# A graph network on one core: deeper edge gather and prefetch, one-word table look-ups in the edge counts, and 16-bit sums in the second edge pass

## The reference, cut to what matters

```python
# x: 3125 nodes x 128, src and dst: 100000 edges, sorted by dst
# layer 0, edge network
h = relu(batchnorm(concat(x[src], x[dst]) @ W1.T + b1))     # statistics over the edges
u = relu(batchnorm(h @ W2.T + b2))
x = layernorm(x + segment_sum(u, dst))
# layer 1, two graph convolutions, along the edges and against them
x = layernorm(x + relu(gcn(x, W_fwd, src, dst) + gcn(x, W_bwd, dst, src)))
# layer 2, four rounds over the edges
h = relu(x @ Wi.T + bi)
for _ in range(4):
    h = h + relu(tanh(aggregate(h @ Weff.T) - relu(h @ (A - A.T).T)))
x = layernorm(x + h)
# layer 3, attention over the edges with 8 heads
x = layernorm(x + attention(x, src, dst) @ Wo.T + bo)
```

## Time and profile before

| what | value |
|---|---|
| median of 3 runs | 4950.45 us (4930.15 to 4968.29) |
| the profiled execution, its own time | 4959.78 us |
| its span, first to last instruction | 4958.1 us |
| PE, DVE, ACT, POOL busy | 3568.6, 2845.3, 1415.5, 935.4 us |
| mean granted TensorE clock | 0.823 of full speed |
| moved by DMA | 657.34 MB, 133 GB/s over the span |

### The profile page before, as it was taken

How to read it: one execution, slowest core, us unless ns; L and a number is a source line. 1 busy time by engine, 2 the same in 40 slices (tenths; PEclk the granted TensorE clock), 3 DMA queues, 4 the chain that set the end, 5 groups by cost and what they waited for, 6 DMA issues and landing times. The chain is left out here.

```text
span 4958.1 us, 85336 instructions
## 1 busy us (share of the span) xinstructions
PE 3568.6 (72%) x18891; PEld 1725.9 (35%) x18992; DVE 2845.3 (57%) x5040; ACT 1415.5 (29%) x1948; POOL 935.4 (19%) x1131
## 2 busy tenths in 40 slices
PE   3666665557787359998887777447779947778994
PEld 2222222243444237777544333312222212222222
DVE  6887777464333123344101111459989949998993
ACT  1123333301222012222101111121138842117880
POOL 2555555454344421111000000100000000000000
PEclk8988889768999679999898999655569975558996
DMA  2344455528998433332484888262213372213331
GB/s 71 110 143 163 171 181 187 185 92 282 318 317 294 146 121 102 97 89 85 93 243 98 189 190 185 53 87 53 53 49 118 126 106 64 53 26 110 116 110 29
DMA packets 808846, 657.34 MB, mean 133 GB/s; under 512 B 599017, under 2 KB 686184, under 8 KB 808516
## 3 DMA queue, kind: packets, MB, share of 16 engines
q1 hardware_dynamic: 677642, 361.12, 27.7%
q10 hardware_dynamic: 106050, 243.93, 14.9%
q0 software_dynamic: 25088, 51.43, 4.0%
HBM read 316.58 MB, written 196.24 MB: 103 GB/s over the span
## 5 line engine op out<-in xcount | busy, mean ns | idle before, releaser
L621 POOL DMA_INDIRECT gat<-a_table,gidx x784 | 791.5, 1010 | 350.8 <-issue 192.4
L1333 DVE CUSTOM_DVE_ANT_0 masked<-psum,mask 128x1564 bf16<-128x1564 f32 x400 | 698.9, 1784 | 196.0 <-PE psum L1670 188.0
L1670 PE MATMUL psum<-qp,kp 96*128 96x391 bf16 x1600 | 589.7, 524 | 304.8 <-DVE mx L1333 158.4
L1368 DVE SCALAR_TENSOR_TENSOR pw<-ex,c_full 128x1564 f32<-128x1564 f32 x400 | 680.8, 1782 | 48.4 <-ACT ex L942 29.8
L1427 PE MATMUL psum<-one_src,one_dst 128*128 x1968 | 455.5, 370 | 306.2 <-issue 151.9
L942 ACT ACTIVATE ex<-psum 128x782 f32<-128x782 f32 x800 | 609.8, 826 | 77.5 <-PE psum L1692 60.7
L1101 DVE TENSOR_SCALAR one_src<-iota_sub,src_low 128x800 f16 x984 | 430.1, 437 | 187.0 <-issue 97.9
L1475 PE MATMUL psum<-c_ring,hp 128*128 128x512 bf16 (+1 forms) x2064 | 422.6, 360 | 77.6 <-DMA c_ring<-c_parts 55.2
L1670 PEld LDWEIGHTS psum<-qp,kp 96*128 x1600 | 174.3, 129 | 719.7 <-issue 719.7
L1256 DVE TENSOR_SCALAR ohd<-iota,dst_c x976 | 221.8, 299 | 327.4 <-PE psum L1596 282.6
L1427 PEld LDWEIGHTS psum<-one_src,one_dst 128*128 x1968 | 197.7, 104 | 569.7 <-issue 504.6
(11 more groups left out here) (318 smaller groups left out, 3379.7 us busy)
## 6 DMA issues: line engine op xcount, KB each, us to landing
c_full<-c_whole SPq DMA_DIRECT2D x80, 977.5 KB, 5.0
a_edges<-gat SPq DMA_DIRECT2D x196, 256.0 KB
a_in<-a_edges ACTq DMA_DIRECT2D x98, 512.0 KB
r_edges<-r ACTq DMA_DIRECT2D x98, 512.0 KB
r_in<-r_edges SPq DMA_DIRECT2D x98, 512.0 KB, 3.5
c_whole<-c_sum ACTq DMA_DIRECT2D x100, 400.0 KB
dst_bc<-dst_half ACTq DMA_DIRECT2D x98, 256.0 KB
c_parts<-c_hi ACTq DMA_DIRECT2D x100, 200.0 KB
```

The source lines that it names most:

```text
L621: g.indirect_dma_start(gat[:, s, 2 * k * P:2 * (k + 1) * P], None, a_table, bass.IndirectOffsetOnAxis(ap=gidx[:, s, k:k + 1], axis=0)).the ...
L1333: v.tensor_tensor_reduce(out=masked[:, n % 2, :].rearrange("p (c t) -> p c t", c=4), in0=psum[:, o:o + 4 * BANK].rearrange("p (c t) -> p c ...
L1368: v.scalar_tensor_tensor(pw[:, step_slot(k), :].rearrange("p (h t) -> p h t", h=HQ), ex[:, step_slot(k), :].rearrange("p (h t) -> p h t", ...
L1670: last = t.matmul(bank((n % 2) * 4 + c, CW), kp[0:KQK, n // 2, ds(b * P, P)], qp[0:KQK, n // 2, ((n % 2) * 4 + c) * CW:((n % 2) * 4 + c + ...
```

## The change

1. **Gather.** In rounds 24 to 48 POOL waits for the group two before instead of the one before, so eight transfers may be under way. The first 24 rounds are as before.
2. **Counts, table.** Preparation packs end and first of a window in one word (`block_tab` row 3). DVE and PE load this word alone and work out the count of pairs done from the window before, for three windows in four; the first of each four loads a second word. ACT loads none: PE sends `window_done` with a one-column matmul of zeros behind each window.
3. **Counts, one-hot.** The two `one_dst` operations of a pair become one `scalar_tensor_tensor` of 256 elements, with two inputs in SBUF.
4. **Pass 1.** `a_in` and `dst_bc` get four buffers, and each load is issued for unit u+4. The loop's body covers four units instead of two.
5. **Pass 2.** `ohd` becomes f16, four buffers, made by one `tensor_tensor` of 1024 elements with two inputs in SBUF. `u` becomes two f16 parts: ACT writes the high part, and a new DVE operation (`low_part`) writes the rest from PSUM; PE waits for that one (`low_ready`). A visit is 16 f16 matmuls with `ohd` as weights, and its sum comes out turned; at the end 25 matmuls turn `y` back. A bound on the values, found in preparation, scales them into the range of f16.
6. Names of semaphores are merged.

```diff
+        a_in = sb("a_in", [P, 4, UE // P, 2, P], f16)
+        u = sb("u", [P, 2, UE // P, 2, P], f16)
+        ohd = sb("ohd", [P, OHD, UE // P, P], f16)          # OHD = 4
...
+        def window(eng, w, done_pairs):
+            word = eng.value_load(block_tab[0:1, 3, ds(w, 1)], min_val=0, max_val=NPAIR * 512 + NPAIR)
+            first = nc.s_assert_within(eng.snap(word & 511), 0, NPAIR - 2)
+            end = nc.s_assert_within(eng.snap(word >> 9), 2, NPAIR)
+            if done_pairs is None:
+                before = eng.value_load(block_tab[0:1, 2, ds(w, 1)], ...)
+            else:
+                before = nc.s_assert_within(eng.snap((done_pairs - first) & 65535), ...)
+            return first, end, before
...
-            def gather(i):
+            def gather(i, most):
                 for s in range(4):
                     after(pool, gat_free[s], i)
-                    after(pool, gathered[(s + 3) % 4], 64 * i + (64 if s >= 1 else 0))
+                    after(pool, gathered[(s - most) % 4], 64 * i + (64 if s >= most else 0))
...
-            gather(0)
-            with pool.Fori(1, NG // 4) as i:
-                gather(i)
+            gather(0, 1)
+            with pool.Fori(1, SLOW_GATHER) as i:              # SLOW_GATHER = 24
+                gather(i, 1)
+            with pool.Fori(SLOW_GATHER, NG // 4) as i:
+                gather(i, 2)
...
             def evict(i, q):
                 w = 4 * i + q
-                before = act.value_load(block_tab[0:1, 2, ds(w, 1)], ...)
-                end = act.value_load(block_tab[0:1, 1, ds(w, 1)], ...)
-                act.wait_ge(S["slot_free"], before + end + PAIRS)
+                act.wait_ge(S["window_done"], w + 1)
...
-                    last = v.tensor_scalar(one_dst[:, ds(slot, 1), t, :], iota_row[:, :],
-                                           row_c[:, ds(p * 2 + t, 1)], window_at[:, ds(w, 1)],
-                                           ALU.subtract, ALU.is_equal)
+                v.scalar_tensor_tensor(one_dst[:, ds(slot, 1), :, :],
+                                       row_c[:, ds(p * 2, 2)].broadcast_to([P, 2, P]),
+                                       window_at[:, ds(w, 1)],
+                                       iota_row[:, :].broadcast_to([P, 2, P]),
+                                       ALU.add, ALU.is_equal).then_inc(S["one_ready"], 1)
...
+                    t.matmul(bank(2 * (q % 2), 1), zerosb[:, 0:P], zerosb[:, 0:1], start=False, stop=True,
+                             skip_group_check=True).then_inc(S["window_done"], 1)
...
+            def low_part(i, s):
+                dve.wait_ge(h2_taken[4], 2 * i + s + 1)
+                v.scalar_tensor_tensor(u[:, s, :, 1, :], psum[:, s * UE:(s + 1) * UE], 0.0, u[:, s, :, 0, :],
+                                       ALU.max, ALU.subtract).then_inc(S["low_ready"], 1)
...
-                        for k in range(UE // P):
-                            last = v.tensor_scalar(ohd[...], iota[:, ds(b * P, P)],
-                                                   dst_c[:, ds(g * (UE // P) + k, 1)], None, ALU.is_equal)
+                    v.tensor_tensor(ohd[:, ds((before + b) & (OHD - 1), 1), :, :],
+                                    iota[:, ds(b * P, P)].broadcast_to([P, UE // P, P]),
+                                    dst_h[:, ds(g * (UE // P), UE // P)].broadcast_to([P, UE // P, P]),
+                                    ALU.is_equal).then_inc(S["agg_ready"], 1)
...
                     for k in range(UE // P):
-                        last = t.matmul(bank(4, P), u[:, s, k * P:(k + 1) * P], ohd[...], ...)
+                        for m in range(2):
+                            last = t.matmul(bank(4, P), ohd[:, ds((before + b) & (OHD - 1), 1), k, :],
+                                            u[:, s, k, m, :], ...)
...
+            pe.wait_ge(S["sums_ready"], 1)
+            for b in range(NB):
+                last = t.matmul(psum[:, b * P:(b + 1) * P], y[:, b * P:(b + 1) * P], identf[:, :], start=True, stop=True)
+            last.then_inc(S["sums_turned"], 1)
```

More of the change, by code:

```diff
@@ L158, in gnn @@
         ab_down = sb("ab_down", [P, 1], i32)
[L159 to L162, removed]
+        bound = sb("bound", [P, 3], f32)
+        expo = sb("expo", [P, 3], i32)
+        scale_up = sb("scale_up", [P, 3], i32)
+        scale_down = sb("scale_down", [P, 3], i32)
         degs = sb("degs", [4, SUB], f32)
@@ L299, in gnn @@
         gat_free = [sem(f"gat_free{s}") for s in range(4)]
-        a_loaded = [sem(f"a_loaded{s}") for s in range(2)]
-        dst_loaded = [sem(f"dst_loaded{s}") for s in range(2)]
+        a_loaded = [sem(f"a_loaded{s}") for s in range(4)]
+        dst_loaded = [sem(f"dst_loaded{s}") for s in range(4)]
         dst_used = [sem(f"dst_used{s}") for s in range(2)]
@@ L1119, in count_four @@
             def count_four(i):
+                done_pairs = None
                 for q in range(4):
                     w = 4 * i + q
-                    first, end, before = window(dve, w)
+                    first, end, before = window(dve, w, done_pairs)
+                    done_pairs = before + end
                     one_hots(w, first, before)
@@ L1443, in count_four_pe @@
             def count_four_pe(i):
+                done_pairs = None
                 for q in range(4):
                     w = 4 * i + q
-                    first, end, before = window_pe(w)
+                    first, end, before = window(pe, w, done_pairs)
+                    done_pairs = before + end
                     after(pe, S["evicted"], w + -1)
@@ L1556, in layer2 @@
                 last.then_inc(h2_psum[3], 1)
-            layer1(0, 0)
-            layer1(0, 1)
+            layer1(0, 0, 0)
+            layer1(0, 0, 1)
             layer2(0, 0)
-            with pe.Fori(1, NU // 2) as i:
-                layer1(i, 0)
-                layer2(i + -1, 1)
-                layer1(i, 1)
-                layer2(i, 0)
+            with pe.Fori(0, NU // 4) as j:
+                for q in (1, 0):
+                    i = 2 * j + (2 - q)
+                    layer1(j + (1 - q), q, 0)
+                    layer2(i + -1, 1)
+                    layer1(j + (1 - q), q, 1)
+                    layer2(i, 0)
             layer2(NU // 2 - 1, 1)
@@ L1595, in sum_edges @@
                     for k in range(UE // P):
-                        last = t.matmul(bank(4, P), u[:, s, k * P:(k + 1) * P],
-                                        ohd[:, ds((before + b) & 1, 1), k * P:(k + 1) * P
-                                            ].rearrange("p o e -> p (o e)"),
-                                        start=(k == 0), stop=(k == UE // P - 1))
+                        for m in range(2):
+                            last = t.matmul(bank(4, P), ohd[:, ds((before + b) & (OHD - 1), 1), k, :].rearrange("p o d -> p (o d)"),
+                                            u[:, s, k, m, :], start=(k == 0 and m == 0),
+                                            stop=(k == UE // P - 1 and m == 1))
                     last.then_inc(S["agg_psum"], 1)
@@ L1621, in _ @@
                                 start=True, stop=True)
-            last.then_inc(S["nd_psum"], 1)
+            last.then_inc(S["map_psum"], 1)
             node_rows(0, x, W["Wfb"], 2 * P)
```

185 lines of the change are left out of this document (100 added, 85 removed).

## The result

The changed kernel takes 4971.07 us (median of 16 runs, 4958.54 to 4986.95) against 4939.41 us for the kernel before (16 runs, 4930.15 to 4968.29): a ratio of 1.0057, interval 1.004 to 1.0073, so it is slower by half a per cent. The profiled execution has a span of 4959.1 us. The forecast was 4676.

The account below looks back on a forecast made before the run. Counts were taken as bound by DVE, pass 1 by the gather in its second part, pass 2 by PE. From 4959.8 us, 188 off through pass 1 and 87 in pass 2 gave 4685, against the median 4676; range 4580 to 4800.

Parts of the forecast that it names:

- 98U + 81G = 356 + 147 = 503 us: Pass 1: DMA time for 98 units (U) and 81 groups (G) left at 1063 us; 553 us at share 0.91.
- A: Rival: the gather gains nothing, its transfers land no faster with eight under way; only pass 2 gains, 4875 us; chance 0.10.
- B: Rival: in pass 2 weights' addresses keep PE's sequencer at 2 us a visit, 97 us stay; 4773 us; chance 0.13.
- C: Rival: in pass 1 four buffers bring the DMA share near 1.0, 503 us instead of 553; 4626 us; chance 0.12.
- D: Rival: denser gathers beside pass 1's loads and stores make each transfer dearer for DMA; about 5060 us; chance 0.04.
- the share of DMA in pass 1 falls well under 0.9 with units over 5.6 us: Pass 1: one of the signs named in advance that the forecast is wrong.
- Nor is the gather (1573): Pass 1: the gather, ending at 1573 us, is not the bound; the DMA engines are, to 1616 us.
- the turn to pass 2: End of pass 1: 25 us added for the turn, so pass 1 ends at 1641 us instead of 1829.
- 84 us of 120: Counts: 120 us saved, 60 from the one-hot and 60 from fewer table loads, range 40 to 190.
- I raised 8.2 us a group to 8.8: Gather beside counts: the new two-input `one_dst` slows POOL to 8.8 us a group, range 8.2 to 10.
- The prediction's upper bound: Total: counts saving only 40 us, together with rival B, reach 4815 us.
- 61 us of 87: Pass 2: 97 us saved on PE by 1.0 us visits, less 10 for the final turn and small operations, net 87.

Follow-up runs that it names:

- e3: Changed kernel with pass 1 of the kernel before (two buffers, two units a loop body), eight transfers from round 24; 4694.85 us, ratio 0.9482.
- k1: Changed kernel with four transfers under way in rounds 30 and 31, eight before and after from round 24; 4715.32 us, ratio 0.9523.
- e2: Kernel before with only the gather's part of the change, eight transfers under way from round 24; 4747.12 us, ratio 0.9589.
- m2: e3 run again word for word in the fifth job; 4979.8 us, ratio 1.0091.
- f3: e3 with eight transfers under way from round 2 on instead of 24; 4867.57 us, ratio 0.9842.
- f0: e3 with the loop bodies of pass 1 doubled to four units on PE, DVE and ACT; 4972.85 us, ratio 1.0061.
- e1: Changed kernel with the old gather put back, four transfers under way in all 49 rounds; 5028.01 us, ratio 1.0166.

## Why the prediction was wrong

*The step that failed* is the one of pass 1: "Left at 1063 are 98U + 81G = 356 + 147 = 503 us; at the share of 0.91, 553 us". It takes for granted that the engines' sequencers keep their pace beside the denser gather, and no rival doubted that: A, B and C never touch it, and D had the right sign and wrong mechanism (the DMA engines are half idle, not overloaded). In the changed kernel's measurement, a starved one, 25 units passed while 80 groups were gathered, and the other 73 had to follow at 4.0 us: 756 us from 1113 to 1869 instead of 553. The prediction's own mark, "the share of DMA in pass 1 falls well under 0.9 with units over 5.6 us", is what the trace shows.

*Where the job is free, the forecast's mechanism holds for most of pass 1, not to its end.* e3 has pass 1 from 1089 to 1614 us, 525 us, with the DMA engines at 0.99 until 1530 (nearer C's 1.0 than my 0.91). From there on the gather ends it, which the prediction had ruled out ("Nor is the gather (1573)") and named as a sign of being wrong: its last copy is at 1594 us, and the last nine units take 84 us with the DMA engines at 0.68:

```profile
1530.00:1614.00 84.00, 49.12 (x241) 25.11 (x241) 17.60 (x40) 10.84 (x9) 47.83 (x59) 0.82 0.68 219
```

That e3 takes 4694.85 us, near 4676, is in part luck: counts end 26 us later than forecast and pass 2 is 15 us longer, while pass 1 is 28 us shorter. The changed kernel itself has not run in a free job. I estimate some 4680 us for it from k1, whose pass 1 the gather ends too: in its row of 1117 to 1209 us 44 POOL operations are 8.8 groups of 10.5 us, so its two rounds with four transfers cost eight times 4.7, 38 us, and 4715 less these is 4677. This is argued, not shown.

*Right:* the turn to pass 2, 24 us for 25, and that the gather's idle time goes. Its end, 1574 to 1580 us for 1573, is luck: the fast rounds began 58 us late (990 for 932), and went at 5.8 us a group for 6.3 to 6.8.

*Counts: right in kind, size off.* 84 us of 120, from one starved trace to another; in free jobs it is 58 (e2 826, e3 768). One new `one_dst` costs 476 ns and DVE's busy time fell from 672 to 636 us, 36 us where I had 69; its idle time before `one_src` fell from 187 to 135 us:

```profile
L1126 DVE TENSOR_SCALAR one_src<-iota_sub,src_low 128x800 f16 x982 | 379.8, 428 | 134.7 <-PE psum L1460 76.6 <-issue 56.5
L1128 DVE SCALAR_TENSOR_TENSOR one_dst<-row_c,window_at,iota_row 128x256 f16 x492 | 234.4, 476 | 0.6 <-issue 0.6
```

*Gather beside counts: sign right, size off.* I raised 8.2 us a group to 8.8; it is 784/82 = 9.6, so that round 24 began at 990 us, not 932. e2, with the old counts, stays at 784/97 = 8.1: the new counts do it. That `one_dst` does it by its two SBUF inputs, as the prediction had it, was not tested by itself. The smaller gain in counts (768 us for 742) is why e3 starts pass 1 at 1089 and not 1063. The changed kernel starts at 1113: its counts take 778 us, and its statistics stage 252 us instead of the 238 forecast, as in m2 (249, 865 to 1114); e3 has 238 in the free job. The prediction's upper bound is summed wrongly: two thirds of 80 us and B's 97 on top of 4676 make 4826, not 4815.

*Pass 2: a size off.* 61 us of 87. A visit's matmuls are 144.7/122 = 1.19 us with 0.45 of idle time before them, where I took 1.0 in all from line 1535 with its fixed moving tile; B's end was 2.0. `low_part` (1.22 for 1.2) and the one-hot (1.37 for 1.2) stayed covered: PE waited 0.4 us for the first and 5.7 for the second.

```profile
L1287 DVE TENSOR_TENSOR ohd<-iota,dst_h (+1 forms) x122 | 165.4, 1372 | 0.0
L1637 PE MATMUL psum<-u,ohd 128*128 128x128 f16 x1952 | 144.7, 225 | 54.4 <-issue 31.5 <-ACT visit_sum L869 17.2 <-DVE ohd L1287 5.7
L1277 DVE SCALAR_TENSOR_TENSOR u<-psum,u 128x1024 f16<-128x1024 f32 x98 | 120.0, 1224 | 212.6 <-ACT u L860 212.6
L1622 PE MATMUL psum<-row,onesb 3*128 3x512 bf16 x193 | 57.3, 375 | 20.9 <-issue 20.5 <-DVE u L1277 0.4
```

*What stays open:* what differs between a starved and a free job (the chip, the time and where the program lies in memory all change with it); by what path the transfers slow the other engines' instructions; and why the rate of the transfers is not all: in the changed kernel eight are under way from 990 us on, but apart from one or two instructions of SP the spells begin at 1106 us, just ahead of pass 1. That more transfers make more of them rests on f3 against f0 in counts, and on pass 1 in starved traces: 13 instructions of 0.5 us or more in 613 us with four (the kernel before, 1182 to 1795), 75 in 467 with eight. That the kernel before stays between 4936 and 4964 us in all six jobs does not say that it is free of them, since its gather, and not its counts, sets the end of its pass 1.

## What to carry to other kernels

Where engines stand idle "on issue" and the DMA engines are not full, look at the sequencer's own rows, for the longest time of an instruction that works on registers alone; and ask whether it comes back in another job before a part of the code is blamed for it. Compare kernels within one job, run the disputed kernel itself in each job, and sort the results by job as well as by kernel: three jobs of mine made clean stories out of a difference that lay in the jobs, and the row that tells them apart was in the first traces. And a gather that shares POOL and the DMA engines with the work it feeds has to be sped up ahead of that work, or a gain in the work can make it later (e1).

## What the runs showed of the hardware that was not expected

- Beside a gather by POOL, the instructions of PE, DVE, ACT and SP can come 0.71 us or 1.42 us apart, in some jobs and not in others, under the same chip number: with eight indirect transfers under way 19.5 against 5.0 us a unit (m2 and e3). POOL's own register instructions never take 0.5 us, and after the gather no engine's does, in any trace.
- With four under way the spells are rarer, not absent: 18 to 42 instructions of 0.5 us or more in the new counts, 79 in the counts of the kernel before, none in any free trace. For the new counts it is 774 to 782 us against 764 to 772, for the old ones 862 against 826.
- Beside pass 1 in the starved jobs PE's granted clock is 0.58 to 0.63, with PE busy 0.38 to 0.49 of the time, and 0.99 in e3's, with PE busy 0.82. The lower clock is not what spaces the instructions: in the statistics stage it is 0.67 to 0.69 in every kernel, without such spells.
- With eight under way the gather goes at 5.8 us a group whether the DMA engines are at 0.52 or 0.99. With four it goes from 8.4 us to 11.6 us when they fill up.
- The best kernel measured in a free job, h3 (changed counts and pass 2, old pass 1, eight transfers from round 2 with one wait a round), takes 4654.91 us, 0.9414 of before. It has not run in a starved job. There f3, the same but for the wait, still gained (0.9842), while e3, with eight only from round 24 on, lost (1.0091): in f3 less of the gather is left when pass 1 begins.
